# Graph network with four message-passing layers: gathers paced by their own landings, and fewer columns on TensorE

## The reference

```python
edge_index = jnp.stack([src, dst])
h = jnp.maximum(_layernorm(x, axis=-1), 0.0)
x = x + _L0_gnn_ref(h, edge_attr_32, src, dst)      # mean over targets of h[src] * pattern, plus h
h = jnp.maximum(_layernorm(x, axis=-1), 0.0)
x = x + _L1_gnn_ref(h, edge_index, L1_gnn_Wq, L1_gnn_Wk, L1_gnn_Wv, L1_gnn_Wo)  # attention over a target's edges
h = jnp.maximum(_layernorm(x, axis=-1), 0.0)
x = x + _L2_gnn_ref(h, L2_gnn_W, src, dst)          # sum of h[src], then @ W
h = jnp.maximum(_layernorm(x, axis=-1), 0.0)
x = x + _L3_gnn_ref(h, edge_index, edge_weight1, edge_attr_3, edge_attr_5, L3_gnn_W)  # tensor product with edge coefficients
```

## Time and profile before

| | us |
|---|---|
| runs, lowest / median / highest | 16094.55 / 16096.28 / 16126.25 |
| span of the profiled execution, first to last instruction | 14816.7 |
| PE busy | 12890.3 (87%) |
| POOL busy | 12431.7 (84%) |
| DVE busy | 9612.6 (65%) |
| ACT busy | 3874.6 (26%) |
| mean granted TensorE clock | 0.948 |

### The profile page before, as it was taken

The page is one execution under the profiler, slowest core; times in us unless marked ns, Lnnn a source line. Parts: engine busy times, 40 slices in busy tenths (PEclk is TensorE's granted clock), DMA queues, the critical chain, the costliest instruction groups (busy, mean ns, idle before and its releaser), DMA issues.

```text
span 14816.7 us, 226154 instructions
## 1 busy us (share of the span) xinstructions
PE 12890.3 (87%) x57644; PEld 10677.8 (72%) x57644; DVE 9612.6 (65%) x13223; ACT 3874.6 (26%) x4265; POOL 12431.7 (84%) x18594
## 2 busy tenths in 40 slices
PE   7999999992699999999689999999769999999996
PEld 6888888881577777777578888888756666767764
DVE  7666666664577777777666666666656665666665
ACT  2222222220233333333222222222211111111111
POOL 6888888887888888888778888888888888888884
PEclk9999999995899999999889999999989999999998
DMA  5444444442344444444345555545433333333332
GB/s 174 148 148 157 157 155 151 149 151 46 101 123 122 124 124 123 122 123 124 90 119 130 129 130 128 131 127 131 110 76 87 86 90 83 90 86 87 87 86 56
DMA packets 1340717, 1727.48 MB, mean 117 GB/s; under 512 B 501932, under 2 KB 1145566, under 8 KB 1339646
## 3 DMA queue, kind: packets, MB, share of 16 engines
q10 hardware_dynamic: 705956, 1154.87, 24.6%
q1 hardware_dynamic: 327194, 407.86, 9.6%
q0 software_dynamic: 306880, 158.96, 7.6%
HBM read 1140.23 MB, written 580.36 MB: 116 GB/s over the span
## 4 chain that ended last, share of the span: by engine, by line
POOL 41%; issue 32%; PE 20%; DVE 5%; POOLq 1%; DMA 0%; DVEq 0%; ACT 0%; ACTq 0%; SPq 0%
POOL rows L492 22%; POOL pace L497 16%; PE psum L690 12%; PE psum L773 7%; POOL outs L509 2%; PE psum L764 2%; DVE work L1340 1%; DVE work L1315 1%; POOLq L496 1%; POOL q_edges L471 1%; POOL work L501 1%; DVE tile_rows L924 0%; DVE work L1323 0%; DVE rows L931 0%; DVE outs L1347 0%
## 5 line engine op out<-in xcount | busy, mean ns | idle before, releaser
L690 PE MATMUL psum<-h_parts,one_hot 128*128 128x448 f32 x49406 | 10813.2, 377 | 482.0 <-ACT one_hot L539 262.4
L690 PEld LDWEIGHTS psum<-h_parts,one_hot 128*128 128x128 f32 x49406 | 9428.8, 192 | 1500.6 <-ACT one_hot L539 313.0
L492 POOL DMA_INDIRECT rows<-h_table,idx x9000 | 8662.9, 963 | 1966.9 <-POOL pace L497 1537.1
L546 ACT ACTIVATE one_hot<-keys 128x896 fp32r<-128x896 bf16 x2533 | 2359.9, 950 | 6435.5 <-PE psum L690 4314.0
L497 POOL MEMSET pace<- 128x288 f32 x9000 | 3213.9, 357 | 18.1 <-issue 13.2
L924 DVE TENSOR_TENSOR tile_rows<-psum,h_mask 128x448 f32<-128x448 f32 x2722 | 1686.2, 619 | 1252.3 <-PE psum L690 991.3
L931 DVE TENSOR_REDUCE rows<-tile_rows 128x32 f32<-128x448 f32 x2722 | 1677.0, 616 | 58.9
L773 PE MATMUL psum<-work,bd_t 128*128 128x512 f32 (+1 forms) x3500 | 1359.2, 514 | 240.1 <-DVE work L1323 141.3
L1323 DVE TENSOR_TENSOR work<-psum,work 128x800 f32<-128x800 f32 x875 | 862.7, 988 | 920.9 <-PE psum L764 864.2
L773 PEld LDWEIGHTS psum<-work,bd_t 128*128 128x128 f32 x3500 | 654.9, 193 | 764.4 <-issue 443.4
L912 DVE TENSOR_REDUCE rows<-psum 128x32 f32<-128x448 f32 x807 | 503.1, 623 | 792.0 <-PE psum L690 741.7
(11 more groups left out here) (202 smaller groups left out, 6198.1 us busy)
## 6 DMA issues: line engine op xcount, KB each, us to landing
keys<-hots ACTq DMA_DIRECT2D x2542, 224.0 KB
keep_in<-keep_flat SPq DMA_DIRECT2D x2000, 100.0 KB
sums<-outs ACTq DMA_DIRECT2D x375, 400.0 KB
rows<-h_table,idx POOLq DMA_INDIRECT x9000
hots<-bit_hot ACTq DMA_DIRECT2D x506, 224.0 KB
hots<-work ACTq DMA_DIRECT2D x506, 224.0 KB
attn<-outs ACTq DMA_DIRECT2D x125, 800.0 KB
edge_in<-pattern_c SPq DMA_DIRECT2D x125, 400.0 KB
```

Of the source, the lines that this page charges most:

```text
L492: nc.gpsimd.indirect_dma_start(out=rows[:, r, j * D:(j + 1) * D], out_offset=None, in_=h_table[:, :], in_offset=bass.IndirectOffsetOnAxis( ...
L546: nc.scalar.activation(one_hots[i % LOOK[l]][:, :, :], loaded_hots[i % BIT_BUFS[l]], ACT.Copy).then_inc(one_hot_cast, 1)
L690: last = nc.tensor.matmul(banks[TILE_BANKS[l][b]][:, 0:H0 * D], one_hots[hot][:, h1, :], h_parts[:, part, h1 * H0 * D:(h1 + 1) * H0 * D], ...
```

## The change

`PE_COLS` goes from 40, 32, 40 and 28 tiles per turn (five chunks) in layers 0 to 3 to 32, 24, 32 and 20, so per chunk from 8, 6.4, 8 and 5.6 to 6.4, 4.8, 6.4 and 4. Pool gathers the remaining columns: 93, 101, 93 and 105 per turn in place of 85, 93, 85 and 97. The memset and the tile `pace` are gone. A gather adds to one of FLYING = 2 semaphores in turn, and before each gather Pool waits until the last gather on the same semaphore has landed. Two gathers ahead of layers 0 and 1 put the first counts on the semaphores. VectorE waits on both semaphores for a chunk's last two gathers.

```diff
-PE_COLS = ((8, 8, 8, 8, 8), (7, 7, 6, 6, 6), (8, 8, 8, 8, 8), (6, 6, 5, 5, 6))
-PACE = 288
+PE_COLS = ((7, 7, 6, 6, 6), (5, 5, 5, 5, 4), (7, 7, 6, 6, 6), (4, 4, 4, 4, 4))
+FLYING = 2
...
-        rows_gathered = [sems(f"rows_gathered{a}_") for a in range(2)]
+        gather_landed = [sems(f"gather_landed{a}_", FLYING) for a in range(2)]
...
+        def landed(l, t, r, j):
+
+            by_pool = [J - n for n in PE_COLS[l]]
+            i = sum(by_pool[0:r]) + j
+            before = sum(TURNS * len(range(i % FLYING, RING * J - sum(PE_COLS[k]), FLYING)) for k in range(l % 2, l, 2))
+            each = 16 * len(range(i % FLYING, sum(by_pool), FLYING))
+            return gather_landed[l % 2][i % FLYING], t * each + 16 * (before + i // FLYING + 2)
...
+                if l < 2:
+                    pool.wait_ge(rows_used[0], l * TURNS + START)
+                    pool.wait_ge(idx_loaded[0], use(l, 0) * 16)
+                    for j in range(FLYING):
+                        nc.gpsimd.indirect_dma_start(
+                            out=rows[:, 0, j * D:(j + 1) * D], out_offset=None, in_=h_table[:, :],
+                            in_offset=bass.IndirectOffsetOnAxis(ap=idx[:, 0, j:j + 1], axis=0)).then_inc(gather_landed[l][j], 16)
...
                         for j in range(J - PE_COLS[l][r]):
+                            slot, n = landed(l, t, r, j)
+                            pool.wait_ge(slot, n - 16)
+                            pool.sem_inc(gather_begun, 1)
                             nc.gpsimd.indirect_dma_start(
                                 out=rows[:, r, j * D:(j + 1) * D], out_offset=None, in_=h_table[:, :],
-                                in_offset=bass.IndirectOffsetOnAxis(ap=idx[:, r, j:j + 1], axis=0)).then_inc(rows_gathered[l % 2][r], 16)
-                            pool.wait_ge(pause_ended, pauses(l, t, r, j))
-                            pool.sem_inc(pause_begun, 1)
-                            nc.gpsimd.memset(pace[:, :], 0.0).then_inc(pause_ended, 1)
+                                in_offset=bass.IndirectOffsetOnAxis(ap=idx[:, r, j:j + 1], axis=0)).then_inc(slot, 16)
...
+            def wait_landed(l, t, r):
+
+                r1, more = r % RING, r // RING
+                for j in range(J - PE_COLS[l][r1] - FLYING, J - PE_COLS[l][r1]):
+                    slot, n = landed(l, t, r1, j)
+                    each = 16 * len(range(gather_landed[l % 2].index(slot), RING * J - per_turn[l], FLYING))
+                    v.wait_ge(slot, n + more * each)
```

More of the change, by code:

```diff
@@ L168, in gnn_kernel @@
         far = work[:, 9, h0_width:h0_width + H0 * D // 2].bitcast(BF16)
-        pace = sb("pace", [P, PACE])
         bit_hots.append(mz[:, CH - H1 * P // 2:CH].bitcast(BF16).rearrange("p (h n) -> p h n", n=P))
@@ L263, in gnn_kernel @@
         x_ready, x_stored = sem("x_ready"), sem("x_stored")
-        pause_begun, pause_ended = sem("pause_begun"), sem("pause_ended")
+        gather_begun = sem("gather_begun")
         block = ctx.enter_context(nc.Block())
@@ L271, in use @@
             return t + (l * TURNS + 1 + more)
-        def gathers(l, t, r, more=0):
-            each = 16 * (J - PE_COLS[l][r])
-            return t * each + (each * (1 + more) + (16 * TURNS * (J - PE_COLS[l - 2][r]) if l >= 2 else 0))
+        def landed(l, t, r, j):
[4 more added lines that the diff above has]
+            return gather_landed[l % 2][i % FLYING], t * each + 16 * (before + i // FLYING + 2)
         per_turn = [sum(c) for c in PE_COLS]
-        def pauses(l, t, r, j):
-            before = sum(TURNS * (RING * J - per_turn[k]) for k in range(l))
-            return t * (RING * J - per_turn[l]) + (before + sum(J - PE_COLS[l][k] for k in range(r)) + j + START)
         tile_base = [sum(TURNS * per_turn[k] + PE_COLS[k][0] for k in range(l)) for l in range(LAYERS + 1)]
@@ L460, in _ @@
         def _(pool):
-            pool.sem_inc(pause_ended, START)
             for l in range(LAYERS):
@@ L945, in pick_next @@
                     pick(l, t, i)
+            def wait_landed(l, t, r):
[4 more added lines that the diff above has]
+                    v.wait_ge(slot, n + more * each)
             def wait_rows(l, t, r):
-                v.wait_ge(rows_gathered[l % 2][r], gathers(l, t, r))
+                wait_landed(l, t, r)
                 v.wait_ge(picked, tile_no(tile_base, l, t, first_tile(l, r + 1)))
@@ L1160, in turn_in @@
                 r1, more = r % RING, r // RING
-                v.wait_ge(rows_gathered[1][r1], gathers(1, t, r1, more))
+                wait_landed(1, t, r)
                 v.wait_ge(picked, tile_no(tile_base, 1, t, first_tile(1, r + 1)))
@@ L1312, in next_rows @@
                 r1, more = (r + 1) % RING, (r + 1) // RING
-                v.wait_ge(rows_gathered[1][r1], gathers(3, t, r1, more))
+                wait_landed(3, t, r + 1)
                 v.wait_ge(picked, tile_no(tile_base, 3, t, first_tile(3, r + 2)))
@@ L1348, in turn_messages @@
                 v.wait_ge(outs_ready[r], use(3, t))
-            v.wait_ge(rows_gathered[1][0], gathers(3, 0, 0))
+            wait_landed(3, 0, 0)
             v.wait_ge(picked, tile_no(tile_base, 3, 0, first_tile(3, 1)))
```

## The result

The change makes the kernel slower: 18580.59 us in the median of three runs (18576.48 to 18582.52) against 16096.28 us, a ratio of 1.153 with a 95% interval from 1.150 to 1.157. The forecast was 19170 us in a range from 17200 to 20600.

A forecast was written before the change was run, and what follows sets the result against it. Pool was taken to set the pace in layer 0, PE close behind everywhere. 9800 gathers x 1.695 us plus 171 gave loops of 16782 us, 3077 more; 16096 + 3077 = 19173, rounded to 19170 us, range 17200 to 20600.

The forecast's parts named there:

- The sign and the mechanism: Layer loops: slower, chance 0.86; period (landing + handoff) / 2 = 1.695 us, longer than the memset's 1.46 us.
- PE's busy time: TensorE's busy time in the changed profile: falls by some 2300 us, less what a lower clock adds.
- The handoff: In Pool's queue, from a landing to the start of the gather that waited for it: 0.79 us, lower bound 0.15.
- The rival that it would be hidden: Pool's sequencer prepares the waiting gather: handoff 0.15 us, period 1.275 us, time 15141 us, faster; chance 0.12.
- The landing: In the loops, from a gather's start until its rows have landed: mean 2.6 us, bounds 2.2 and 3.0.
- The turn ends: First gather of a turn takes 3.85 us, the second follows after 1.25: costs 1.71 us per turn, 171 us for 100.
- I carry it over unchanged: The runs' median lies 1279.6 us above the profiled span, unexplained by any row; kept in the forecast time.
- TensorE's clock: Rival: TensorE, busy only in bursts, falls to 1.2 GHz in the loops; time 19904 us; chance 0.12.
- the reading: Profile of the kernel before: no VectorE instruction before a gather; other stops are "issue", 295 us in 107 cases.
- what Pool needs: Pool's period for gathers without memset, as in the node stages: 0.94 us each and 0.30 between them, 1.25 us.

The follow-up runs named there:

- e14: The change with each gather waiting for the one just before it, so one in flight: 33580.54 us in one run.
- third group: Four runs on one chip: the kernel before with three longer memsets (15023.65, 15210.93, 15795.34 us), and e14; the kernel before took 14811.26 us there.
- first two groups: Two groups of four runs varying waits, columns, gathers in flight and memset; the kernel before took 16115.30 and 16218.23 us on their chips.
- e9: The kernel before, memset kept, with TensorE columns between the old and new tables (36, 28, 36, 24 tiles per turn): 16101.20 us, ratio 0.992.
- e2: The kernel before, memset kept, with the change's new columns: 16012.24 us, ratio 0.994.
- e1: The change's new wait with the columns of the kernel before: 17677.64 us, ratio 1.098.
- e6: The kernel before with the change's columns and a memset of 528 columns in place of 288: 17744.25 us, ratio 1.093.
- e3: The change with three gathers in flight in place of two: 19588.65 us, ratio 1.215.
- e5: The kernel before without the memset and its wait, gathers back to back: 21430.90 us, ratio 1.330.
- e7: The kernel before with a memset of 144 columns in place of 288: 20784.42 us, ratio 1.281.
- e10: The change with three gathers in flight and the memset of 288 columns put back behind each gather: 16718.46 us, ratio 1.030.

## Why the prediction was right, and where it was off

- **The sign and the mechanism** were right: landing plus handoff over two is the period, the loops hold all of the loss, Pool is 53% busy (about 55% forecast), and VectorE waits for rows in every layer, up to 17 us per chunk (2163 us over layer 0's 125) where some 10 were forecast. The idle time before gathers was to end with landings; the profile shows it for 4805 of 8318 us. PE's busy time fell by 1719 us and not by 2300: the lower clock gave the rest back, as the forecast had reserved.
- **The handoff** was taken as 0.79 us; from landing to start it is 0.78 in the change and 0.77 in e14. The rival that it would be hidden is refuted in the chain.
- **The landing** was taken as 2.6 us for the mean, with the remark that values are skewed upwards. With one gather in flight (e14) that is about right, 2.52. In the change it is longer: the mean of 3.58 less 0.77 for the handoff is 2.8 us. That lies in the tail, for the typical landing is 2.4 us; of the sums of two steps one in four is over 3.75 us and one in twenty over 5.18. So the period within a chunk was 1.78 in place of 1.695, and the loops took 17481 in place of 16782 us, 699 more.
- **The turn ends** came as described and a little cheaper: the first gather of a turn starts 3.1 to 3.5 us after the last one of the turn before (3.85 forecast), the second 1.25 to 1.34 us later. Against two mean steps of 3.56 that is about 1.0 us per turn, 100 us in all and not 171.
- **The step that failed** is "I carry it over unchanged", the 1279.6 us between the profiled span and the runs. After the change a run is 2.6 us longer than its span. The third group shows what the number was: the kernel before takes 14811 us on one chip and 16115 or 16218 on two others, and its profile fits the first. What the change adds is 3764 us to that profile and 2484 to the runs. The two errors have opposite signs, 699 us too little in the loops and 1277 too much in the carried part, and this is why 19170 came within 3.2% of 18581. That closeness is luck. Without the carried part the same sum gives the span as 17894, 684 us short of the 18578 measured, which would still have been in the range; with the true loops and the 1279.6 carried it would have been about 19870.
- **Where the 1280 us went** is argued and not shown. On the chips of the first two groups the kernel before is slower than its cadence asks for, and fewer tiles take the surplus away: against the profiled 14817 us plus 1.49 us for each added gather, e9 (9400 gathers) has some 690 us too much and e2 (9800) none, an estimate from their steps. (The profiled execution of e2, with TensorE on its chain, took 220 us more than its median.) That fits a TensorE which is behind on those chips and waits for nothing once Pool's period is 1.78 us.
- **TensorE's clock** fell as the rival said, from 0.97 in the loops to between 0.78 and 0.83, and it cost nothing at the end: PE has 0 or 1% of the chain in the change, in e1 and in e6. In e2, where it has 43%, a lower clock may cost something; that wasn't measured.
- Among what stops a gather in the kernel before, the reading left out 134 us in three waits for `idx`. They change nothing in the sum.
- What the prediction didn't see is the true use of the memset. It called 1.25 us what Pool needs, as if a shorter period could only help; e3, e5 and e7 show that at 1.26 to 1.37 us the kernel loses 21 to 33%.

## What to carry to other kernels

When a gather waits for an earlier one, work out (landing + handoff) / in flight from rows of the same queue, and take the mean with its tail, not the usual value. A pause that looks like waste may protect another engine: shorten it in steps, and look for gaps between instructions that wait for nothing. Before you add a difference between profile and runs to a sum, find out whether both came from the same chip.

## What was not expected of the hardware

- Indirect gathers of 128 rows at one per 1.25 to 1.35 us go with TensorE's weight loads coming 2.1 us apart and more in places, for stretches of many microseconds, with no wait in the program and the DMA engines 12% busy in the stretch shown. At 1.47 us the number of such gaps differs by kernel and chip: none in the kernel before, 4 in e10, 232 in e9 and 376 in e2. At 1.51 us and above there is none. That the instructions themselves arrive late is argued from the gaps; no row names what they wait for.
- The same kernel, paced by the same memset, takes 14811 us on one chip and 9% more on two others. The natural guess is that those two chips have such gaps at before's cadence. The 376 and 232 gaps of e2 and e9 speak for it, but there is no profile of the kernel before from these chips, so it stays open.
- A second gather in flight hardly lengthens a typical landing: a median of 3.21 us for two steps in the change, 3.15 us for one step in e14. The tail is what makes the mean: even alone in flight a gather can take 7.1 us.
